# Last stage of a two-layer transformer kernel: eight subtractions on GpSimd, ahead of 32 indirect sends or spread between them

## What is computed

```
scores = softmax(xf @ router_w)
expert_weights, top_experts = top_k(scores, 2)
for k in range(2):
    # tokens sorted by their k-th expert, at most `capacity` each: xe [8, capacity, 128]
    h  = gelu(einsum('ech,ehf->ecf', xe, w1))        # w1 [8, 128, 512]
    ye = einsum('ecf,efh->ech', h, w2)               # w2 [8, 512, 128]
    out = out + scatter(ye) * expert_weights[:, k]
x = x + gb * (out + bias)
```

## Time and profile before

| | |
|---|---|
| median of 3 runs | 1941.07 us (1940.59 to 1944.42) |
| profiled execution, span | 1941.6 us |
| PE busy | 1570.5 us (81%) |
| POOL busy | 1254.4 us (65%) |
| DVE busy | 1201.4 us (62%) |
| ACT busy | 790.3 us (41%) |
| instructions | 26551 |

### The profile page before, as it was taken

One profiled execution on the slowest core, in us unless ns is written; L12 is line 12 of the kernel. 1 busy time (PEld: TensorE's weight loads), 2 busy tenths in 40 slices (PEclk: granted clock), 3 DMA queues, 4 the chain that ended last, 5 costly groups with the idle time before them and its releaser, 6 DMA issues. The chain is left out here.

```text
span 1941.6 us, 26551 instructions
## 1 busy us (share of the span) xinstructions
PE 1570.5 (81%) x8882; PEld 1082.6 (56%) x8882; DVE 1201.4 (62%) x2510; ACT 790.3 (41%) x1347; POOL 1254.4 (65%) x1057
## 2 busy tenths in 40 slices
PE   5899999999999999999999889999656654448570
PEld 3556556755567656566656678888312322337560
DVE  6876676657666656665663255666599899441034
ACT  2245444354443444433444343322578653213120
POOL 4588899789887888887897542100266586570616
PEclk7799999999999999999999999999788766568785
DMA  6223221122122221221120200000355453222213
GB/s 172 66 77 92 52 66 47 38 60 66 34 50 61 51 49 35 65 67 38 39 66 12 64 1 1 1 1 1 97 152 146 126 141 94 84 87 70 80 49 84
DMA packets 93560, 125.30 MB, mean 65 GB/s; under 512 B 13664, under 2 KB 53492, under 8 KB 93424
## 3 DMA queue, kind: packets, MB, share of 16 engines
q1 hardware_dynamic: 89328, 115.58, 23.6%
q0 software_dynamic: 4096, 8.02, 1.4%
HBM read 56.56 MB, written 16.78 MB: 38 GB/s over the span
## 5 line engine op out<-in xcount | busy, mean ns | idle before, releaser
L835 DVE CUSTOM_DVE_ANT_0 ring<-ring,mask 128x128 f32<-128x128 f32 (+7 forms) x512 | 383.5, 768 | 187.1 <-PE ring L697 186.6
L921 ACT ACTIVATE prob<-ring 128x512 f32<-128x512 f32 x576 | 315.0, 597 | 296.4 <-PE ring L712 293.0
L975 POOL TENSOR_TENSOR acc<-acc,prob 128x512 f32<-128x512 f32 x272 | 353.0, 1298 | 72.1 <-ACT prob L921 48.3
L728 PE MATMUL ps_o<-prob,v 128*64 128x256 f32 x2304 | 281.8, 386 | 4.2 <-issue 3.8
L697 PE MATMUL ring<-k,x 128*128 128x512 f32 (+3 forms) x768 | 250.1, 405 | 36.6 <-ACT prob L921 22.0
L711 PE MATMUL ring<-x,k 128*128 128x512 f32 x576 | 258.5, 449 | 24.6 <-DVE neg_m L835 15.4
L712 PE MATMUL ring<-x,k 128*128 128x512 f32 x576 | 229.4, 398 | 0.0
L697 PEld LDWEIGHTS ring<-k,x 128*128 128x128 f32 x768 | 136.7, 197 | 144.3 <-ACT prob L921 49.9
L728 PEld LDWEIGHTS ps_o<-prob,v 128*64 128x64 f32 x2304 | 154.2, 137 | 106.2 <-issue 38.4
L972 POOL TENSOR_TENSOR acc<-prob 128x512 f32<-128x512 f32 x144 | 184.9, 1284 | 8.8 <-ACT prob L921 7.4
L942 POOL TENSOR_TENSOR other<-other,sin 128x512 f32<-128x512 f32 x96 | 136.2, 1419 | 57.3 <-DVE other L814 56.7
(11 more groups left out here) (319 smaller groups left out, 3096.5 us busy)
## 6 DMA issues: line engine op xcount, KB each, us to landing
x<-other SPq DMA_DIRECT2D x256, 128.0 KB, 2.4
m_x_rep<-u_mem SPq DMA_DIRECT2D x59, 512.0 KB
x<-rot SPq DMA_DIRECT2D x128, 128.0 KB, 2.4
slots_in<-zeros SPq DMA_DIRECT2D x2, 2048.0 KB, 8.7
slots_out<-wo SPq DMA_DIRECT2D x16, 256.0 KB
gate<-slots_in SPq DMA_DIRECT2D x11, 256.0 KB
m_x_rep<-u_mem SPq DMA_DIRECT2D x10, 256.0 KB
e_w<-in_w SPq DMA_DIRECT2D x3, 704.0 KB, 7.1
```

The source lines that it names most:

```text
L728: mm = e.matmul(ps_o[s * D:(s + 1) * D, qb % 2 * 2 * P:(qb % 2 + 1) * 2 * P], v[g % 2][:, kb, :], prob[i % NPROB][:, s * 2 * P:(s + 1) * 2 ...
L835: e.tensor_tensor_reduce(ps, ps, mask_1[:, SEQ - n:SEQ], 1.0, -3.0 * NEG, ALU.add, ALU.min, neg_m[g % 2][:, c, h, qb % QPC:qb % QPC + 1]). ...
L921: e.activation(prob[i % NPROB][:, :], banks(("s2",) + key, BANK), ACT.Exp, scale=-1.0).then_inc(s2_exp.sem, 1)
L975: e.tensor_tensor(total[:, :], total[:, :], tile[:, :], ALU.add).then_inc(summed.sem, 1)
```

## The change

POOL makes the low halves of experts 0 and 1 before it waits for the slots of the second choice. The other six it makes one at a time, after the sends 4, 8, 12, 16, 20 and 24 of the second choice; the last eight sends follow each other. The instructions are the same in number and shape, and so are their waits (each low half waits for its high half). No other engine's list is changed.

```diff
     def gpsimd(self, e):
         for c in range(self.n):
-            cc = slice(c * self.width, (c + 1) * self.width)
-            e.wait_ge(self.hi_done, c + 1)
-            e.tensor_tensor(self.lo[:, cc], self.src[:, cc], self.hi[:, cc].bitcast(F32), ALU.subtract).then_inc(self.lo_done, 1)
+            self.rest(e, c)
+
+    def rest(self, e, c):
+        cc = slice(c * self.width, (c + 1) * self.width)
+        e.wait_ge(self.hi_done, c + 1)
+        e.tensor_tensor(self.lo[:, cc], self.src[:, cc], self.hi[:, cc].bitcast(F32), ALU.subtract).then_inc(self.lo_done, 1)
@@ capacity_experts
         def gpsimd(e):
             for i in range(TILES - TPB, TILES):
                 send(e, first, h, slots_in, 0, i, sent)
-            w_split.gpsimd(e)
+            w_split.rest(e, 0)
+            w_split.rest(e, 1)
             e.wait_ge(second.slotted, 1)
             for i in range(TILES):
                 send(e, first, h, slots_in, 1, i, scattered[1])
+                if i % 4 == 3 and i // 4 + 2 < E1:
+                    w_split.rest(e, i // 4 + 2)
             e.wait_ge(got_zero, 1)
```

## The result

The changed kernel takes 1910.91 us (median of 4 runs, 1909.90 to 1912.89) against 1940.83 us for the kernel before beside it (4 runs): a ratio of 0.984, with a 95% interval of 0.983 to 0.985. That is 30 us less, 1.6% by the ratio. The profiled execution's span is 1911.2 us.

A forecast was written before the change was run, and what follows sets the result against it. It took the moment when PE's completions are let through again, not POOL's own work, as the bound. From the span of 1941.6 us it took 3 x 6.78 = 20.3 us, forecasting 1921 us, range 1908 to 1947.

The forecast's parts named there:

- the likeliest case: POOL's pauses between sends let PE's completions through; 1914 to 1930 us, chance 0.40.
- The early start: Ahead of the sends: two subtractions instead of eight, slots 7.35 us earlier at about 1702.3, first send at 1703.0.
- the prediction's lock: VectorE and GpSimd port pair, held exclusively for a whole instruction; claimed to agree with d_weight's 8.10 us.
- The end of the sends: POOL's last send ends at 1750.9 to 1752.9, against 1750.94 before; POOL gains nothing.
- What bounds the phase: In the last stage, when PE's completions are let through again, not POOL's work; one unexplained piece of 32.13 us.
- The price of a pause: Four sends leave about 0.75 us of backlog, less than a POOL pause of 1.23 to 1.56 us.
- The experts gained: PE stands three experts further when its completions are let through: 3 x 6.78 = 20.3 us gained.
- The release: PE's completions are let through 1.5 to 4.7 us after POOL's last send, at 1753.5 to 1757.
- The hold in the last eight sends: Without pauses there, PE's completions get stuck again 6 us or so in, at 1748.
- Full relief: Rival: PE's completions hardly held even in the last eight sends; 33 us less, 1908 us, chance 0.07.
- The slower case: Rival: no pause helps, earlier sends hold PE earlier in its work; 1947 us, 1951 at worst, chance 0.21.
- Its second part: A POOL subtraction stands behind DVE's 6.88 us memset of c_got, with all later sends: up to 6.9 us more.

The follow-up runs named there:

- the second experiment: Against the kernel before: low halves 0 and 1 on POOL, the other six on DVE behind the slots, sends without a pause; 1937.25 us, ratio 0.996.
- the short pauses: Against the kernel before: low halves 2 to 7 on DVE, POOL subtraction of 160 columns instead of 512 after sends 4, 8, ... 24; 1925.84 us, ratio 0.992.

## Why the prediction was right

The time, 1910.91, lies in the range of 1908 to 1947, and the sign and mechanism are those of the likeliest case; but it lies under that case's own range of 1914 to 1930. The forecast of 1921 gained 20.3 us, the measurement 30. That the time lies in a range of 39 us, which holds gains and losses, says little; what supports the mechanism are the marks below and the experiments.

- The early start. Slots at 1702.70 instead of 1709.62, first send at 1703.48, d_weight down from 8.10 to 0.75 us: as worked out. By itself this is worth little, as the second experiment shows. The 8.10 us were a wait behind some six subtractions in a row, more than the one instruction for which the prediction's lock is held: DVE did not get in between them.
- The end of the sends, forecast at 1750.9 to 1752.9: 1751.20.
- What bounds the phase: right. It is when PE's completions are let through, not POOL's own work, and the runs show it by adding and taking away pauses.
- The price of a pause. The step that took 0.75 us of backlog behind four sends, from the 1.5 us behind eight in the earlier trace rows, was not measured itself; that 0.55 us was too short and 1.3 us enough agrees with it.
- The experts gained, the term that was mis-sized: three forecast, four measured. I took 6.78 to 9 us for an expert and the return of the hold at 1748 as the end of PE's progress. The pace was 6.78 us throughout, completions being at most 0.8 us later than usual (ACT idle 3.35 us ahead of the first result, 2.55 later). The first c_dn group ended at 1721.0, not 1722: PE's high clock came three matmuls earlier in the first c_up group than in the kernel before, and the group's last matmul was not late. And in the last eight sends PE itself was not slowed (clock 1.00, matmuls on time to 1751.3), only its completions were late. So the fifth group was done by 1748.1 and four experts were gained, 4 x 6.78 = 27.1 us.
- The release. Forecast 1753.5 to 1757, measured 1752.81 and so below that range, 1.6 us behind the last send, about as behind the eight sends of the earlier trace rows (1.5), against 4.7 us in the kernel before. The next c_dn starts 1756.40 - 1753.55 = 2.85 us earlier. 27.1 + 2.85 = 30.0 us, the measured gain. The first gather, forecast near 1786, starts at 1776.50 for the same reasons.
- The hold in the last eight sends came about when forecast: the group that ended at 1748.1 was seen at 1752.81.
- Rivals. Full relief (1908) came close in time, but it is the hold in the last eight sends that it denies, and that is there. The slower case needed that no pause lifts the hold. Its second part, a subtraction stuck behind DVE's memset, did not happen: the subtraction at 1720.91 ran its 1.30 us inside the memset of 6.88 us. The Trainium skill (SBUF — State Buffer, "SBUF: two separate sides") has VectorE take the shared pair in a 2-port performance mode or with two inputs in SBUF; this memset has no input, and the trace shows that it doesn't keep a subtraction waiting.

What stays open is where PE's completions wait. The runs show that it is tied to POOL's indirect DMAs in a row, that sends to DRAM and gathers from it both do it, that ACT's completion is not held (in the kernel before PE starts at 1840.10, 0.15 us after ACT's copy ends, in the midst of the gathers), and that the DMA engines are mostly idle meanwhile (share 0.15). They don't show the queue itself, nor whether the gaps or the lower mean rate of the sends bring the relief. Nor does any run tell whether it would be there without the profiler.

## What to carry to other kernels

When another engine seems to wait for nothing that the trace shows, and its producer's record ended long ago, look for a long run of indirect DMAs on GpSimd at that time. Break such a run into groups of four with a gap of about 1.3 us, best filled with work that has to be done anyway, and keep the gaps off the path on which the last of the DMAs is waited for. Here this was worth 30 us at the sends, 3 to 7 of them for the earlier start, and 29 us more at the gathers.

## What the runs showed of the hardware

- 32 indirect DMAs without a gap, one every 1.28 us (1.30 for gathers), bring PE from 13.5 to 1.2 instructions per us (2.0 beside the gathers), 13.7 us behind the first send and 9.7 us behind the first gather, and its completions reach others up to 31.5 us late. PE's granted clock falls from 1.00 to 0.50 in it, from the level of 2.4 GHz to that of 1.2 GHz, and the first group afterwards, which begins at 0.50, takes 5.5 us instead of 3.6.
- The tail from the last send's end to the release is 1.5 us behind eight, 1.6 us behind the last eight of the changed kernel (1.7 in two experiments with pauses), and 4.5 to 4.7 us behind 32. With the short pauses it is 0.8 us, though the hold lasts longer there than in the changed kernel, so the tail is not a measure of the hold.
- A send is itself slower beside some work of DVE. In the five runs where DVE makes the six low halves (3.69 us in one go, two inputs in SBUF), the first two sends, which run beside them, take 1.30 and 1.48 us instead of 0.97 to 0.99. These are the sends of the run with seven pauses:

```profile
1703.49 1.30 POOL L1249 DMA_INDIRECT slots_in<-attn_t,f_slot  x1 [2.47 <-DVE f_slot L1244]
1705.09 1.48 POOL L1249 DMA_INDIRECT slots_in<-attn_t,f_slot  x1 [0.30 <-issue]
1706.87 0.97 POOL L1249 DMA_INDIRECT slots_in<-attn_t,f_slot  x1 [0.30 <-issue]
```
